# A preparation stage rewritten: keys made in their packed field, row normalisation on ScalarE, bonus product on GpSimd

## The reference, cut to what matters

```python
delta = shifted - h
xr, xw, xk, xv, xa = (h + delta * x_m for m in "r w k v a")
r = xr @ W_r ;  k = xk @ W_k ;  v = xv @ W_v
log_w = -softplus(-(tanh(xw @ w_lora_a) @ w_lora_b + w_lora_bias)) - 0.5
a = sigmoid(xa @ a_lora_a @ a_lora_b + a_lora_bias)
g = sigmoid(r @ g_lora_a) @ g_lora_b + g_lora_bias
kk = (k * k_k) per head of 16, divided by its norm
k = k * (1.0 + (a - 1.0) * k_a)
# the scan takes r, log_w, k, v, -kk, kk * a
bonus = (r * k * r_k).sum(-1) * v      # per head
```

## Time and profile before

| what | us |
|---|---|
| median of 3 runs | 4454.21 (4453.38 to 4456.28) |
| the profiled execution | 4475.04 |
| its span, first to last instruction | 4473.3 |
| of this, `prepare`: first DMA issue to the first of the recurrence | 1762.4 to 2278.0, 515.6 |
| VectorE busy in `prepare` | 415.9 |
| TensorE busy in `prepare` | 399.3 |
| ScalarE busy in `prepare` | 224.1 |
| GpSimd busy in `prepare` | 90.8 |

### The profile page before, as it was taken

The page is one execution under the profiler, slowest core; times in us unless marked ns, Lnnn a source line. Parts: engine busy times, 40 slices in busy tenths (PEclk is TensorE's granted clock), DMA queues, the critical chain, the costliest instruction groups (busy, mean ns, idle before and its releaser), DMA issues. The chain is left out here.

```text
span 4473.3 us, 72079 instructions
## 1 busy us (share of the span) xinstructions
PE 3935.0 (88%) x23448; PEld 2685.1 (60%) x23448; DVE 3218.0 (72%) x8707; ACT 2194.9 (49%) x7361; POOL 2060.3 (46%) x1668
## 2 busy tenths in 40 slices
PE   5999999999996696988849999999999999936598
PEld 2344444444435464666638888888888888835466
DVE  5777777877745111789869999999999999946310
ACT  2666666666665211444404565555655555613211
POOL 2211211211223421111248888888888888725422
PEclk7999999999996798999979999999999999967699
DMA  4322332332346232244342323232322223166232
GB/s 111 82 74 70 100 79 70 87 88 63 79 96 214 74 128 84 104 169 169 150 102 31 42 34 43 34 42 34 41 35 39 37 36 41 15 181 219 80 127 80
DMA packets 479034, 378.41 MB, mean 85 GB/s; under 512 B 298378, under 2 KB 440997, under 8 KB 472544
## 3 DMA queue, kind: packets, MB, share of 16 engines
q1 hardware_dynamic: 466400, 348.90, 32.0%
q0 software_dynamic: 12288, 25.28, 1.7%
HBM read 222.13 MB, written 159.58 MB: 85 GB/s over the span
## 5 line engine op out<-in xcount | busy, mean ns | idle before, releaser
L750 DVE TENSOR_REDUCE at_neg_max<-at_slot 128x1 f32<-128x512 f32 (+3 forms) x1216 | 745.8, 655 | 247.5 <-PE at_slot L542 244.4
L672 ACT ACTIVATE at_prob<-at_slot 128x512 f32<-128x512 f32 (+1 forms) x1216 | 632.4, 579 | 354.3 <-PE at_slot L562 353.4
L2157 PE MATMUL sc_added<-sc_outer,sc_ident 128*128 128x128 f32 x4096 | 585.5, 286 | 78.8 <-POOL sc_outer L1908 58.0
L2157 PEld LDWEIGHTS sc_added<-sc_outer,sc_ident 128*128 128x128 f32 x4096 | 496.4, 191 | 209.3 <-DVE sc_state L2058 115.0
L1921 POOL TENSOR_TENSOR sc_terms<-sc_seen,sc_pack 128x1024 f32<-128x1024 f32 (+2 forms) x288 | 604.7, 2151 | 13.7 <-PE sc_ps_o L2179 13.7
L2179 PE MATMUL sc_ps_o<-sc_terms,sc_ident 128*128 128x256 f32 x2048 | 607.0, 381 | 2.1 <-POOL sc_terms L1921 2.1
L390 POOL TENSOR_SCALAR_AFFINE_SELECT at_prob<-at_prob 128x512 f32<-128x512 f32 x256 | 162.9, 636 | 888.2 <-ACT at_prob L672 888.0
L2081 ACT ACTIVATE sc_seen<-sc_state 128x512 f32<-128x512 f32 x256 | 153.1, 598 | 749.1 <-DVE sc_decayed L2022 740.2
L542 PE MATMUL at_slot<-at_k_stack,at_q_stack 96*128 96x512 bf16 (+3 forms) x1536 | 459.4, 335 | 22.0 <-DMA at_k_stack<-parts 19.5
L1908 POOL TENSOR_TENSOR sc_outer<-sc_pack 128x2048 f32<-128x2048 f32 x128 | 467.3, 3672 | 5.0
L562 PE MATMUL at_slot<-at_q_stack,at_k_stack 99*128 99x512 bf16 (+3 forms) x1536 | 452.7, 331 | 12.2 <-ACT at_prob L672 11.8
(11 more groups left out here) (306 smaller groups left out, 7155.8 us busy)
## 6 DMA issues: line engine op xcount, KB each, us to landing
packed<-pr_pack SPq DMA_DIRECT2D x16, 3072.0 KB, 13.4
sc_pack<-packed SPq DMA_DIRECT2D x512, 96.0 KB, 3.6
parts<-at_parts SPq DMA_DIRECT2D x96, 256.0 KB
f_up_w<-in_ffn_wi SPq DMA_DIRECT2D x16, 1024.0 KB
f_down_w<-in_ffn_wo SPq DMA_DIRECT2D x16, 1024.0 KB
at_q_stack<-parts SPq DMA_DIRECT2D x32, 384.0 KB
at_k_stack<-parts SPq DMA_DIRECT2D x32, 384.0 KB
slots<-at_no_row SPq DMA_DIRECT2D x2, 4128.0 KB
```

The lines of the kernel that those rows point to most:

```text
L672: act.activation(prob[:, first:first + n, q1 - tiles * P:q1], ps[:, 0:n * tiles * P].rearrange("p (n k) -> p n k", n=n), ACT.Exp)\
L750: dve.tensor_reduce(neg_max[:, chunk, qt, h:h + n], ps[:, 0:n * tiles * P].rearrange("p (n k) -> p n k", n=n), AX.X, ALU.max, negate=True) ...
L2157: pe.matmul(added[h][:, 0:HALF], ident[:], outer[m % 2][:, 2 * n + s, h * HALF:(h + 1) * HALF], start=(s == 0), stop=False)
```

## The change

- The loops of `prepare` are written out: 7 turns as straight code on each engine, with constants in the waits.
- `normalise` becomes `stats` (VectorE), `root` (ScalarE), `affine`: a reciprocal and a small product on VectorE, then 8 activations of 128x256 on ScalarE.
- The biases of w and a become a 65th row of the second lora matmul, against a row of ones. ScalarE takes both sigmoids straight from PSUM; VectorE's four additions go.
- ScalarE copies k from PSUM to its packed field; VectorE makes `kk` and the key from there. The key waits for `kk`, since it is written over its own input.
- The bonus product goes to GpSimd; VectorE keeps the reduction (`dots`).
- The packed fields are stored as soon as they are complete, ahead of the bonus.
- The list of jobs has another order: `w_inner` lies ahead of `turn_r`, `w` ahead of `g_inner`, the next x is transposed after `v`, the mix for a comes one turn ahead, between the two halves of `key`.

```diff
-PREPARE_USER = {... "w": "dve", "a_inner": "act", "g": "dve", "a": "dve", "v": "act", "k": "dve"}
+PREPARE_USER = {... "w": "act", "a_inner": "act", "g": "dve", "a": "act", "v": "act", "k": "act"}
-    return [("normalise", 0), ("turn_x", 0), ("turn_x", 1), ("mix", "r"), ("mix", "w")]
+    return [("stats", 0), ("root", 0), ("affine", 0), ("turn_x", 0), ("turn_x", 1), ("mix", "r"), ("mix", "w"), ("mix", "a")]
-    return (halves("r") + halves("turn_r") + [("w_inner", 0), ("g_inner", 0), ("mix", "a")]
-            + plus([("normalise", 0)]) + halves("w") + [("mix", "v"), ("a_inner", 0)] + halves("g") + halves("a") + [("mix", "k")]
-            + plus(halves("turn_x")) + halves("v") + plus([("mix", "r")]) + halves("k")
-            + halves("key") + plus([("mix", "w")]) + halves("bonus"))
+    return (halves("r") + [("w_inner", 0)] + halves("turn_r") + halves("w") + [("g_inner", 0), ("a_inner", 0), ("mix", "v")]
+            + plus([("stats", 0)]) + halves("g") + halves("a") + plus([("root", 0), ("affine", 0)]) + [("mix", "k")]
+            + halves("v") + plus(halves("turn_x") + [("mix", "r")])
+            + halves("k") + plus([("mix", "w")]) + [("key", 0)] + plus([("mix", "a")]) + [("key", 1)]
+            + halves("dots") + halves("bonus"))
...
-            with eng.Fori(0, BATCH - 1) as b:
+            for b in range(BATCH - 1):
...
 # SyncE, after the gate stores and the load of x
+                for h in range(2):
+                    slots.wait_read(sp, ("v", h), alone=True)
+                    sp.wait_ge(chain, 1 + b * TURN + 5 * (h + 1))
...
+                    sp.dma_start(packed[rows]...).then_inc(pack_stored[h], 16)
                 for h in range(2):
                     sp.wait_ge(bonus_ready, 1 + b * 2 + h + 1)
...
 # GpSimd
-                        pool.wait_ge(bonus_ready, 1 + b * 2)
+                        pool.wait_ge(dots_ready, 1 + b * 2)
...
+                    elif stage == "bonus":
+                        pool.wait_ge(dots_ready, 1 + b * 2 + what + 1)
...
+                        pool.tensor_tensor(by_head(bonus[what][:]), field(what, FV), dots[what]..., ALU.mult)
 # ScalarE
+                    elif stage == "affine":
+                        act.wait_ge(affine_ready, 1 + f + 1)
+                        for n in range(TILES):
+                            act.activation(xn[:, n, :], x[:, n, :], ACT.Identity, bias=shift[:, n:n + 1],
+                                           scale=rstd[:, n:n + 1]).then_inc(xn_ready, 1)
...
+                    elif stage == "k":
+                        act.activation(field(what, FK), by_head(ps[:]), ACT.Copy).then_inc(emptied[s], 1)
...
-                        slots.wait_read(act, (stage, what))
-                        act.activation(z["w"][what][:], z["w"][what][:], ACT.Sigmoid).then_inc(z_used, 1)
+                        act.wait_ge(w_packed, 1 + b * 2)
+                        act.activation(z["w"][what][:], ps[:], ACT.Sigmoid).then_inc(emptied[s], 1)
 # VectorE
-                        for t in range(TILES):
-                            dve.tensor_scalar(xn[:, t, :], x[:, t, :], mean_var[:, t, 0:1], rstd[:, t:t + 1],
-                                              ALU.subtract, ALU.mult).then_inc(xn_ready, 1)
+                        dve.scalar_tensor_tensor(out=shift[:], in0=rstd[:], scalar=-1.0, in1=mean_var[:, :, 0],
+                                                 op0=ALU.mult, op1=ALU.mult).then_inc(affine_ready, 1)
...
-                        dve.tensor_tensor(by_tile(kk[:]), by_tile(ps[:]), wide_of["k_k"], ALU.mult)\
+                        dve.tensor_tensor(by_tile_head(kk[:]),
+                                          field(what, FK).rearrange("p (n h) d -> p n h d", h=HEADS),
+                                          wide_of["k_k"].rearrange("p n (h d) -> p n h d", d=D), ALU.mult)\
                            .then_inc(kk_ready, 1)
+                        dve.wait_ge(kk_ready, 1 + b * 2 + what + 1)
                         dve.scalar_tensor_tensor(out=field(what, FK), in0=by_head(scaled[:]), scalar=1.0,
-                                                 in1=by_head(ps[:]), op0=ALU.add, op1=ALU.mult)\
+                                                 in1=field(what, FK), op0=ALU.add, op1=ALU.mult)\
```

More of the change, by code:

```diff
@@ L2265, in prepare @@
         r_turned = sb("r_turned", [P, KC, T])
-        inner = {"w": sb("w_inner", [RW, T]), "a": sb("a_inner", [RW, T]), "g": sb("g_inner", [RG, T])}
+        inner = {"w": sb("w_inner", [RW + 1, T]), "a": sb("a_inner", [RW + 1, T]), "g": sb("g_inner", [RG, T])}
         HW = HALF_TILES * C
@@ L2369, in _ @@
             load_x(1)
-            with sp.Fori(0, BATCH - 2) as b:
+            for b in range(BATCH - 2):
                 store(turn_counts(turn, b), b, b + 2)
@@ L2381, in _ @@
             own.up(pool.memset(turned[:], 0.0))
+            own.done()
+            for m in "wa":
+                own.link(pool.memset(inner[m][RW:RW + 1, :], 1.0))
             own.link(pool.memset(ident[:], 0.0))
@@ L2397, in part @@
                     elif stage == "key":
-                        slots.wait_read(pool, ("k", what))
+                        pool.wait_ge(key_ready, 1 + b * 2 + what + 1)
                         pool.wait_ge(rr_ready, RR_FIRST + b * 4 + what + 1)
@@ L2401, in part @@
                             .then_inc(rr_ready, 1)
+                    elif stage == "bonus":
+                        pool.wait_ge(dots_ready, 1 + b * 2 + what + 1)
+                        slots.wait_read(pool, ("v", what))
+                        pool.wait_ge(bonus_stored[what], 1 + b * 16)
+                        pool.tensor_tensor(by_head(bonus[what][:]), field(what, FV),
+                                           dots[what][:].unsqueeze(2).broadcast_to([P, HALF_TILES * HEADS, D]),
+                                           ALU.mult).then_inc(bonus_ready, 1)
             run(pool, part)
@@ L2567, in part @@
                         mix(slots, what)
-                    elif stage in ("w", "a"):
-                        slots.wait_filled(dve, s, use)
-                        if stage == "w":
-                            dve.wait_ge(w_packed, 1 + b * 2)
-                        else:
-                            dve.wait_ge(z_used, 1 + b * 4)
-                        dve.tensor_tensor(by_tile(z[stage][what][:]), by_tile(slot[s][:]), wide_of[stage], ALU.add)\
-                           .then_inc(emptied[s], 1)
                     elif stage == "g":
@@ L2582, in part @@
                     elif stage == "key":
-                        s, use = slots.plan.place["k", what]
-                        ps = slot[s]
-                        slots.wait_filled(dve, s, use)
-                        dve.wait_ge(z_used, 1 + b * 4 + 2 + what + 1)
+                        slots.wait_read(dve, ("a", what), ("v", what), ("k", what))
                         own.up(dve.scalar_tensor_tensor(
@@ L2607, in part @@
                                                           in1=by_head(a_sig[what][:]), op0=ALU.mult, op1=ALU.mult))
[L2608 removed]
+                    elif stage == "dots":
                         dve.wait_ge(rr_ready, RR_FIRST + b * 4 + 2 + what + 1)
                         dve.wait_ge(bonus_ready, 1 + b * 2)
[L2611 to L2616 removed]
+                        dve.tensor_reduce(dots[what][:], by_head(rr[what][:]), AX.X, ALU.add).then_inc(dots_ready, 1)
                 assert b is None or own.n == TURN, own.n
```

68 lines of the change are left out of this document (36 added, 32 removed).

## The result

The changed kernel takes 4476.21 us (median of 5 runs, 4473.0 to 4478.54), the kernel before 4455.36 in 5 runs beside it (4453.38 to 4456.28): a ratio of 1.0048, 95% interval 1.0038 to 1.0059. It is slower by 20.9 us. The forecast was 4492, with a range of 4461 to 4514.

What follows compares the result with a forecast made beforehand. VectorE's own throughput was taken to bound the kernel before. First turn +12.4, six periods +37.4, last turn -2.2 and end -9.8 sum to +37.8 us, giving 4492 us on the median of 4454.21; range 4461 to 4514.

Steps and rivals of the forecast that it cites:

- The ring K to F to K: One turn walked through the engines' queues, K to next K: 64.2 us forecast, from 61.5 to 65.7, against 57.96 before.
- K: The start of the second key half on VectorE; the forecast counts a turn's times from it.
- F: The time at which TensorE has filled the slot of a, half 1; forecast at K+30.2, range K+27.5 to K+31.7.
- from F to the next K: ScalarE's sigmoid, affine, packing and x copies, then VectorE's delta, mixes and first key half: 34.0 us.
- Rival (a): Busy time decides after all: the turn near TensorE's own 48.5 us, 4397 us in total; chance 0.07.
- (d): Period stays tied to VectorE's list: 58 us, total within 0.2%; chance 0.06 together with a weaker form of Rival (a).
- Signs that did not come: Expected in the profile: second key halves 63 to 65 us apart, TensorE waiting some 10 us for r's rows.
- From K to F: Key, root, r copies, transposes, five matmul groups: 30.2 us, including 1.4 for half clock (0 to 2.9).
- Straight code: Within From K to F: writing out the loop brings transposes from K+7.34 to K+7.0, 0.3 us a turn.
- GpSimd: Its bonus product slows VectorE's mix for v by 2.1 us, hidden by 7 us of slack before g.
- First turn, last turn, end: The stage outside the six periods: first turn +12.4 us, last turn -2.2, end -9.8.
- Rival (b): TensorE stays at half clock through w and g_inner after idling: 3.6 us more each turn, 4518 us; chance 0.06.

Runs made afterwards that it cites:

- e2: The changed kernel with the bonus product back on VectorE, after dots: 4477.23 us, ratio 1.0049 to the kernel before.
- e1: The changed kernel with the 8 normalising operations back on VectorE, same place in the list: 4468.12 us, ratio 1.0031 to the kernel before.
- e3: The changed kernel with root and affine moved up in the list, ahead of g: 4470.02 us, ratio 1.0031 to the kernel before.
- e4: As e3, and the transposes of the next x and their copies moved ahead of v: 4427.40 us, ratio 0.9937 to the kernel before.
- e12: e9 with the next rows' statistics first in VectorE's list and the mix for v behind the reciprocal: 4415.04 us, ratio 0.9862 to the kernel before.
- e6: The changed kernel with r's matmuls and copies one turn ahead, between the two key halves: 4494.65 us, ratio 1.0091 to the kernel before.
- e8: The changed kernel with the stores in the old order, bonus before packed fields: 4487.00 us, ratio 1.0070 to the kernel before.
- e5: The kernel before with only its preparation loops written out as straight code: 4459.29 us, ratio 1.0008 to the kernel before.
- e9: e4 with r, w_inner and the transposes of r one turn ahead, between the key halves: 4436.40 us, ratio 0.9921 to the kernel before.
- e11: e3 with w_inner's matmuls done three times: 4489.50 us, ratio 1.0041 to the kernel before.
- e10: e4 with w_inner's matmuls done twice: 4449.14 us, ratio 0.9950 to the kernel before.

## Why the prediction was right, step by step, and which term was off

**The mechanism.** The ring K to F to K, as predicted, is what the rows show: transposes at K+7.1 (7.0), affine at F+3.05 (F+3.1) and 4.04 us (4.07), VectorE's waits 9.20 (9) and 4.81 (5), from F to the next K 33.5 us (34.0). e2 shows that VectorE's freed time is worth nothing. e1 shows that ScalarE's 4 us of affine are worth 3 us in a clean turn, e3, e4 and e12 that the order of jobs is worth 3, 7 and, in all, 10.6 us. Rival (a), busy time decides, is refuted for this order of jobs, and (d) too. The condition of (a), r's rows ahead of the last root, is not enough either: e6 fulfils it and its turns are 64 us. With all the ties moved that e12 moves, a turn is 51 us, still not 48.5.

**Signs that did not come.** Second key halves were to be 63 to 65 us apart and were 61.5 to 62.0. TensorE was to wait some 10 us for r's rows and waited 8.54: r's own matmuls took 8.74 to 8.83 us instead of the 7.07 assumed, partly at half clock behind 2.51 us of idle time. That lies ahead of the wait and costs nothing.

**The mis-sized term** is the clock loss in "From K to F". I took 1.4 us for w at half clock, between 0 and 2.9 (the rows give 2.5; nothing gives the rest). In all seven turns w had nearly full clock (3.62 to 3.81 us long). With 0.2 us less for the transposes and 0.2 for the five groups, K to F was 28.4 us in this turn, not 30.2; F to K gave 0.5. The mean turn was 61.6 instead of 64.2: six times 2.6 are 15.5 us, of which the clock term is 1.4 of each 2.6 and the rest is spread over the others. In the last turn K to F was 27.9, by the same terms, and the turn 2.4 shorter than forecast. Together this is the difference between 37.8 and 21.0 but for 1 us at the two ends. The rows that I weighed came from a kernel in which TensorE idled 0.8 to 1.1 us between the transposes and the next matmuls; now w follows at once. Whether that makes the difference no run tells: it follows at once in e1 and e3 too. The full clock was no chance of one execution: e2 and e8, with the same list of jobs, had it in all their turns (w 3.62 to 3.78). e1 and e3 show, in 3 of 7 turns each, that the loss, when it comes, is larger than my upper bound: w at 7.03 and g_inner at 4.84 make 4.6 us, not 2.9.

**Straight code** [step "From K to F"] was given 0.3 us a turn; e5's clean turns (57.1) are 0.2 to 0.5 shorter than the clean ones before (57.3 to 57.6), so it was about right. The rows show where a part of it was: in six turns before, ScalarE's copies of r began 0.23 to 0.25 us late by a wait that is put down to issue (1.4 us in all), and e5 has no such wait. The mean of before, 57.96, is no measure for that, since it holds the turn of 60.58 with half clock.

**GpSimd.** The forecast for the mix for v was 4.6 us, it took 4.91, and the products stayed hidden. But the cover of 7 us that I named was nearly used up: 2.4 went to the mix, 1.0 to the small operation after the statistics, which also meets GpSimd (1.16 us) and which I had not counted, and g came 1.5 earlier, at K+23.3. VectorE was through at K+21.0: 2.3 us of cover left, the wait of 2.26 ahead of the gate above. The Trainium skill (SBUF — State Buffer, section "Who interferes with whom") says that a VectorE instruction with one SBUF input is free of GpSimd unless it is of a kind, such as `tensor_scalar`, that can take both ports. The trace agrees: the statistics take 2.70 us beside GpSimd and 2.71 at the start of the stage without it, while the tensor-scalar behind them (1.16 us beside GpSimd's product, 0.17 without) ends at 1859.94, as that product does (1854.26 and 5.65 us long).

**First turn, last turn, end.** +12.8 (12.4), -4.6 (-2.2, K to F again), -9.1 (-9.8). e8 undoes the last and loses 10.1. Two slips in the sums change little: 61.5 less the 1.4 us of a cheaper affine is 60.1, not 60.3, and seven times 3.6 is 25, not 26.

**Rival (b)**, the clock at half through w and g_inner, did not happen in the changed kernel, and happened in its neighbours: in e1 and e3 in some turns, in e6 in all. Its price against full clock was 4.4 to 5 us a turn in e1 and e3, which is the 1.4 of the sum and the 3.6 of the rival together, and 5.1 us or more in e6 (w 7.16, g_inner 5.20 to 6.09 instead of 3.62 and 3.60). So 0.06 for it was probably too small. That the changed kernel escaped it is luck as far as the prediction goes: nothing that I can show explains it.

## What to carry to other kernels

When one written list is the queue order of every engine, the length of a turn can be set by a ring of waits through these queues, as in the changed kernel, and not by the busy time of the fullest engine. Before moving work to an idle engine, write down what stands behind it in that engine's queue and who waits for that; e4 gives back 49 us to the changed kernel by order alone, and though ScalarE loads two tables more in each turn. And when a tie is cut, read the job next behind the one that was moved, since it inherits the wait (e6: w_inner behind the root; e9: the statistics behind the keys).

## What the runs showed of the hardware that I had not expected

**TensorE's clock after idle time.** The view by stretch of e3 (columns as in the earlier trace rows; the number behind GpSimd's count is the granted clock, 0.50 is 1.2 GHz and 1.00 is 2.4 GHz): the transposes and then w of two successive turns, both after 10.23 us of idle time and in the same order.

```profile
1840.50:1843.80 3.30, 3.30 (x16) 3.30 (x17) 3.23 (x3) 3.03 (x3) 0.00 (x0) 0.50 0.03 11
1843.90:1847.30 3.40, 3.40 (x17) 3.01 (x17) 3.40 (x4) 3.19 (x3) 3.32 (x2) 1.00 0.99 407
1899.40:1902.80 3.40, 3.40 (x16) 3.40 (x17) 3.33 (x4) 3.07 (x3) 0.00 (x0) 0.50 0.06 23
1902.90:1909.60 6.70, 6.70 (x17) 5.24 (x17) 6.70 (x6) 3.33 (x3) 6.69 (x3) 0.50 1.02 410
```

In one the clock rose as the transposes ended, in the next it stayed low for all of w, 7.03 us. e1 and e11 show the same two kinds, and e10 one such turn. The long turns of e5 and of the kernel before are another: the clock falls in the middle of a turn, in a_inner_b's matmuls, behind 1.1 to 1.2 us of idle time. What tells them apart stays open: not the idle time (2.6 to 10.2 us gave both), and not the work before it, which is the same in each turn. The Trainium skill (TensorE: Matmul & The Clock Gate, section "Part 4: PE-mode transpose") says that transposes don't count as busy in the way of other matmuls. Here w began at full clock right behind 3.4 us of transposes in all seven turns of the changed kernel that have idle time ahead of them, and in e6, where w itself came first after 7.2 to 8.9 us of idle time with no transposes between, w took 7.16 or 7.17 us, half clock throughout, in all seven. Set side by side these speak against it; the long turns of e1 and e3, with w at half clock behind the same transposes, would fit it. No run settles it.

**Small operations of VectorE beside GpSimd.** An operation on 128x8 values took 0.17 us alone and 1.16, 1.71 and 1.80 us beside GpSimd's product; the mix for v took 4.91 instead of 2.48. In e12 two such operations lie on the ring, and together they are 3.2 us longer than alone, more than a two-input operation on 128x1024 values takes (1.22 us).

**The groups differ.** The kernel before took 4455 to 4456 us beside e1 to e8, on two chips, and 4474 and 4477 beside e9 to e12, on two others. In the profiles the difference lies ahead of this stage: it began at 1742.9 to 1745.6 us in e1 to e8 and at 1760.9 to 1763.8 in e9 to e12 (1762.4 in the profile of the kernel before). So ratios within a group, and lengths inside the stage, are to be compared, and times across groups are not. Whether the chip itself makes the difference no run shows.
